# Rope on even and odd tiles without a shuffle, and TensorE's side work behind every second score step

## The chip, the cores and the metric

The kernel runs on one core of one Trainium2 chip. The metric is the device time of one execution in microseconds (us). The three runs of the kernel before took 2365.91, 2367.55 and 2371.05 us; their median is 2367.55 us.

## The reference

A macaron block on x of shape (32 samples, 512 positions, 256 features): half a routed feed-forward layer, attention, half a feed-forward layer again. The change touches attention alone.

```python
def rotate_half(x):
    x1 = x[..., ::2]
    x2 = x[..., 1::2]
    return jnp.stack((-x2, x1), axis=-1).reshape(x.shape)
...
freqs = jnp.exp(-math.log(10000.0) * jnp.arange(0, DH, 2) / DH)      # DH = 16, 16 heads
angles = jnp.repeat(pos[:, None] * freqs[None, :], 2, axis=-1)
qkv = x @ Wqkv.T
...
q = cos * q + rotate_half(q) * sin
k = cos * k + rotate_half(k) * sin
scores = where(causal, q k^T / 4, -inf)
out = softmax(scores) @ v
return out @ Wo.T                                                    # x is added by the caller
```

## The kernel before, in words

`program` builds tables, then runs `ffn_phase`, `attention_phase`, `ffn_phase`, one after the other. Only `attention_phase` (from L504) and the tables that `kernel` makes on the host differ after the change.

**Slots.** Attention goes through the samples in a software pipeline written out by hand. A slot is one group G of four heads of one sample; a sample s has four slots, g = 0 to 3. In its `slot` function each engine has its own list for the slot, and the engines meet only in semaphores. In slot G, TensorE computes what the row maxima need of group G (`max_scores`, L883), the transposed scores of group G-2 (`scores`, L907), probabilities times V of group G-3 (`probs_v` with kt 1, 3, 2, L927) and the first such product of group G-2 (kt 0). A slot has 11 steps n. Steps 0 to 9 have one score step into one of two banks `st_ps`; steps 0 to 10 have one maximum step into one of three banks `mx_ps` (`MX_BANK`). Score step c waits for the exponential c-2 (its bank), and maximum step n for the maximum that used its bank before: step 2 for maximum 0, 3 for 1, 5 for 2, 6 for 3, 8 for 5, 9 for 6, 10 for 7, and in the next slot 0 for 8 and 1 for 9.

**The turn.** At step 1 `turn_maxima` (L876, matmul at L880) transposes the maxima of the group before. It waits for `max_done` 11 G: all 11 maxima of that slot. ScalarE copies the result (`mneg`, L843), and a DMA writes it as a row into the query stack.

**VectorE** reduces each maximum step (`maxima`, L753), in order, and has between them: `begin_rope` (L722), `rope_low` (L730), `normalise_output` (L758: a reciprocal and a product), the statistics of the sample after next (L99 to L111, in slot 2 behind maximum 1), `low_of` (L774) of the transposed input and of the transposed attention output, and `add_residual` (L803). **ScalarE** computes ten exponentials (`exps`, L818) and has copies between them: the high halves of rope (`rope_high`, L820), of the transposed input and output (`high_of`, L828), V (`v_copy`, L860), and `o32` (L848), which `turn_output` (L982) waits for. **GpSimd** masks the probabilities in four instructions a slot (L675), and in `rope` (L678) makes the sine product (L681) and the sum (L685) of one tile. **SyncE** issues all DMAs in order: it writes the rotated queries and keys as fp16 high and low halves to a DRAM image (L646 for q, L655 for k) once `qk_lo` says that they are there, and reads each image back into the stacks in six requests (`read_stack`, L603, issued at L608). The maximum step 0 of slot 0 waits for the new sample's q and k stacks.

**Rope before.** The q and k of the next sample are four PSUM tiles t = 0 to 3 (q, q, k, k), each 128 features x 512 positions, two projected in slot 0, two in slot 1 (`project_qk`, L944, two halves of three matmuls each). Even and odd features stand beside each other in the partitions. VectorE multiplies the tile by the cosine and shuffles neighbouring partitions into `swapped`:

```python
nc.vector.tensor_tensor(by_cos[t % 2][:], x_ps[t % 2][:], cos_t[:], ALU.mult)
nc.vector.stream_shuffle(swapped[t % 2][:], x_ps[t % 2][:], [i ^ 1 for i in range(32)]).then_inc(rope_in, 1)
```

GpSimd multiplies `swapped` by a signed sine and adds. ScalarE rounds the sum to fp16 (L824), VectorE takes the rest (L734).

**TensorE's other work before** (`slot`, L1016): a half projection (slots 0 and 1; a V projection, L960, in slot 2) behind steps 0, 1, 4 and 5, the turn behind 1, three `probs_v` behind 2, `turn_output` behind 5, `probs_v` kt 0 behind 8. In slot 3 the transposes of the input (L973) stand behind 0, the transposes of the output (`transpose_o`, L990) behind 4, and two output projections each (`project_o`, L1004) behind 9 and 10.

Of the kernel before, what the change touches and what calls it, by code (L numbers as in the profile page):

```python
# [503 lines left out]
def attention_phase(nc, tab, src, dst, cos, sin):  # L504
# [10 lines left out]
    with ExitStack() as ctx:  # L515
# [13 lines left out]
        swapped = [sb(f"swapped{i}", [P, T], F32) for i in range(2)]  # L529
# [27 lines left out]
        xT_lo, qk_done, rope_in, sin_done = sem("xT_lo"), sem("qk_done"), sem("rope_in"), sem("sin_done")  # L557
        rope_done, qk_hi, qk_lo, v_done = sem("rope_done"), sem("qk_hi"), sem("qk_lo"), sem("v_done")
# [40 lines left out]
        def _(sp):  # L599
# [69 lines left out]
        def _(pool):  # L669
# [8 lines left out]
            def rope(n, t):  # L678
                idx = 4 * n.b + t
                pool.wait_ge(rope_in, idx + 1)  # L680
                nc.gpsimd.tensor_tensor(by_sin[t % 2][:], swapped[t % 2][:], sin_t[:], ALU.mult).then_inc(sin_done, 1)  # L681

                wait(pool, qk_lo, idx - 1)
                pool.wait_ge(sin_done, idx + 1)
                nc.gpsimd.tensor_tensor(rotated[t % 2][:], by_cos[t % 2][:], by_sin[t % 2][:], ALU.add).then_inc(rope_done, 1)  # L685
# [3 lines left out]
            def slot(s, g):  # L689
# [4 lines left out]
                if g < 2 and sample(s + 1):  # L694
                    rope(s + 1, 2 * g)
# [17 lines left out]
                if g < 2 and sample(s + 1):  # L713
                    rope(s + 1, 2 * g + 1)
# [3 lines left out]
        def _(dve):  # L718
# [3 lines left out]
            def begin_rope(n, t):  # L722
# [4 lines left out]
                nc.vector.tensor_tensor(by_cos[t % 2][:], x_ps[t % 2][:], cos_t[:], ALU.mult)  # L727
                nc.vector.stream_shuffle(swapped[t % 2][:], x_ps[t % 2][:], [i ^ 1 for i in range(32)]).then_inc(rope_in, 1)  # L728
# [49 lines left out]
            def slot(s, g):  # L778
                G = 4 * s.b + g
                for n in range(11):  # L780
                    if group(G):
                        maxima(s, g, n)
                    if g in (1, 2) and sample(s + 1) and n in (0, 3):
                        rope_low(s + 1, 2 * (g - 1) + (n == 3))
                    if group(G - 3) and n == 5:
                        normalise_output(s, g)
                    if g < 2 and sample(s + 1) and n in (2, 6):
                        begin_rope(s + 1, 2 * g + (n == 6))
# [5 lines left out]
                    if g == 3 and sample(s + 2) and n in (1, 2):  # L794
                        low_of(xT.lo, xT.hi, s + 2, n - 1, xT_hi, xT_lo)
                    if g == 3 and sample(s + -1) and n in (5, 7):
                        low_of(oT.lo, oT.hi, s + -1, int(n == 7), oT_hi, oT_lo)
# [14 lines left out]
        def _(act):  # L812
# [12 lines left out]

            act.wait_ge(consts_set, 2)
# [5 lines left out]
            def slot(s, g):  # L832
                G = 4 * s.b + g
                for n in range(10):
                    if group(G - 2):
                        exps(G, [n])
                    if g in (1, 2) and sample(s + 1) and n in (0, 2):
                        rope_high(s + 1, 2 * (g - 1) + (n == 2))
# [5 lines left out]
                    if group(G - 3) and n == 3:  # L844
# [4 lines left out]
                    if g == 3 and sample(s + 2) and n in (0, 1):  # L849

                        wait(act, v_done, 2 * (s + 2).b)
                        high_of(xT.hi, s + 2, n, xT_done, xT_hi)
                    if g == 2 and sample(s + 1) and n in (4, 7):
                        v_copy(s + 1, int(n == 7))
                    if g == 3 and sample(s + -1) and n in (4, 5):

                        wait(act, o_done, 2 * (s + -1).b)
                        high_of(oT.hi, s + -1, n - 4, oT_done, oT_hi)
# [13 lines left out]
        def _(pe):  # L872
# [143 lines left out]
            def slot(s, g):  # L1016
# [4 lines left out]
                before = group(G - 3)  # L1021
                for n in range(11):
# [4 lines left out]
                    if n == 2 and before:  # L1027
                        probs_v(s, g, 3, 1, 1)
                    if n == 1 and group(G - 1):
                        turn_maxima(s, g)  # L1030
                    if n == 2 and before:
# [78 lines left out]
```

## Time and profile before

| what | value |
|---|---|
| median of three runs | 2367.55 us |
| time of the profiled execution | 2366.41 us |
| its span, first to last instruction | 2364.7 us |
| busy, TensorE matmuls | 2146.5 us, 91% |
| busy, VectorE | 1919.6 us, 81% |
| busy, ScalarE | 1358.4 us, 57% |
| busy, GpSimd | 1276.5 us, 54% |
| mean granted TensorE clock | 0.975 |
| rope cosine product, shuffle (L727, L728), means | 678, 733 ns |

A busy matmul is not a matmul at its peak: the records of successive matmuls overlap, because each record has its drain in it. So below, work is priced by the distance from one start to the next, not by durations; the same holds for VectorE and ScalarE, where a record of 0.68 us is followed 0.60 us after its start by the next.

### The profile page before, as it was taken

What the parts mean: (1) busy time and instruction counts of PE and PEld (TensorE: products, weight loads), DVE (VectorE), ACT (ScalarE), POOL (GpSimd) and SP (SyncE); (2) the same over time, 40 slices, a digit from 0 to 9 for tenths busy, and PEclk for the clock granted to TensorE, in tenths of its full rate; (3) what the DMA queues carried; (4) which work ended last, traced back from release to release, by engine and by line L of the source; (5) the groups of instructions that cost most, each with busy time, mean ns of one, the idle gap of its engine ahead of it and who ended that gap; (6) DMA issues with size and microseconds to landing.
All of it is one profiled execution on the core that took longest, in us unless ns stands there. A gap on an engine that the chain in (4) does not pass through costs nothing. (4 is left out here: it accounts for less than half of the span.)

```text
span 2364.7 us, 53376 instructions
## 1 busy us (share of the span) xinstructions
PE 2146.5 (91%) x18188; PEld 1163.7 (49%) x18188; DVE 1919.6 (81%) x3961; ACT 1358.4 (57%) x2567; POOL 1276.5 (54%) x1459
## 2 busy tenths in 40 slices
PE   2999999589999999999999999999999986999999
PEld 1666666324444444444444444444444433666666
DVE  4777777469989998998998999899899855777776
ACT  2555555136666676666666666666666663455453
POOL 3666666335545554554554555455455425666664
PEclk9999999679999999999999999999999987999999
DMA  5566666333444454444454445444444413666664
GB/s 157 179 200 200 202 202 202 97 66 89 94 96 91 94 102 94 90 96 89 98 96 92 91 97 101 91 90 97 94 99 95 77 37 128 201 201 200 202 201 163
DMA packets 280350, 295.31 MB, mean 125 GB/s; under 512 B 45744, under 2 KB 263184, under 8 KB 280080
## 3 DMA queue, kind: packets, MB, share of 16 engines
q1 hardware_dynamic: 279536, 290.85, 48.6%
q8 instruction: 146, 2.39, 0.5%
q14 instruction: 124, 1.02, 0.2%
q10 hardware_dynamic: 544, 1.05, 0.1%
HBM read 140.08 MB, written 83.89 MB: 95 GB/s over the span
## 5 line engine op out<-in xcount | busy, mean ns | idle before, releaser
L818 ACT ACTIVATE at_probs<-at_st_ps 128x512 f32<-128x512 f32 x1280 | 748.1, 604 | 468.7 <-PE at_st_ps L923 462.1
L753 DVE TENSOR_REDUCE at_mx<-at_mx_ps 128x1 f32<-128x512 f32 (+3 forms) x1408 | 838.0, 633 | 142.9 <-PE at_mx_ps L905 142.9
L675 POOL TENSOR_SCALAR_AFFINE_SELECT at_probs<-at_probs 128x512 f32<-128x512 f32 x512 | 319.0, 635 | 679.2 <-ACT at_probs L818 675.4
L923 PE MATMUL at_st_ps<-at_q_stack,at_k_stack 49*128 49x512 f16 (+3 forms) x2048 | 461.3, 303 | 73.0 <-ACT at_probs L818 70.9
L900 PE MATMUL at_mx_ps<-at_k_stack,at_q_stack 48*128 48x512 f16 (+3 forms) x2048 | 493.8, 304 | 21.0 <-DMA at_k_stack<-qk_image 11.5
L431 ACT ACTIVATE f_h<-f_h_ps,f_b1s 128x512 f32<-128x512 f32 x256 | 176.0, 688 | 358.6 <-PE f_h_ps L473 347.1
L923 PEld LDWEIGHTS at_st_ps<-at_q_stack,at_k_stack 49*128 49x128 f16 x2048 | 136.6, 94 | 462.1 <-ACT at_probs L818 338.8
L905 PE MATMUL at_mx_ps<-mask,turn 64*128 64x128 bf16 (+2 forms) x1408 | 342.6, 243 | 0.0
L940 PE MATMUL at_pv_ps<-at_probs,at_v 128*32 128x512 f32 (+3 forms) x4096 | 333.7, 444 | 0.0
L489 PE MATMUL f_y_ps<-f_w2hi,f_hhi 128*128 128x256 f16 x1024 | 279.2, 273 | 0.0
L489 PE MATMUL f_y_ps<-f_w2lo,f_hhi 128*128 128x256 f16 x1024 | 279.2, 273 | 0.0
L489 PE MATMUL f_y_ps<-f_w2hi,f_hlo 128*128 128x256 f16 x1024 | 279.2, 273 | 0.0
L473 PE MATMUL f_h_ps<-f_xThi,f_w1hi 128*128 128x512 f16 x512 | 197.5, 386 | 31.2 <-DVE f_xTlo L380 31.1
L99 DVE BATCH_NORM_STATS2 f_stats<-f_x 128x6 f32<-128x256 f32 x256 | 89.8, 413 | 143.6 <-DMA f_x<-after_attention 72.7
L473 PE MATMUL f_h_ps<-f_xThi,f_w1lo 128*128 128x512 f16 x512 | 197.0, 385 | 0.0
L473 PE MATMUL f_h_ps<-f_xTlo,f_w1hi 128*128 128x512 f16 x512 | 196.6, 384 | 0.0
L681 POOL TENSOR_TENSOR at_by_sin<-at_swapped,at_sin 128x512 f32<-128x512 f32 x128 | 175.4, 1370 | 35.8 <-DVE at_swapped L728 35.8
L900 PEld LDWEIGHTS at_mx_ps<-at_k_stack,at_q_stack 48*128 48x128 f16 x2048 | 158.6, 94 | 68.5 <-DVE at_mx L753 38.7
L685 POOL TENSOR_TENSOR at_rotated<-at_by_cos,at_by_sin 128x512 f32<-128x512 f32 x128 | 180.6, 1411 | 19.1 <-POOL at_by_sin L681 0.4
L389 DVE TENSOR_TENSOR f_hlo<-f_h,f_hhi 128x512 f16<-128x512 f32 x256 | 172.0, 728 | 19.0 <-ACT f_hhi L432 18.9
L340 POOL TENSOR_TENSOR f_res<-f_x,f_b2q 128x1024 f32<-128x1024 f32 x64 | 150.8, 2357 | 64.6 <-DMA after_ffn<-f_res 31.6
L327 POOL TENSOR_SCALAR f_xn<-f_x,f_ve,f_rstd 128x256 f32<-128x256 f32 x256 | 169.7, 674 | 13.0 <-issue 12.1
(117 smaller groups left out, 3903.1 us busy)
## 6 DMA issues: line engine op xcount, KB each, us to landing
at_q_stack<-qk_image SPq DMA_DIRECT2D x192, 128.0 KB, 4.5
at_k_stack<-qk_image SPq DMA_DIRECT2D x192, 128.0 KB, 4.7
f_x<-in_x SPq DMA_DIRECT2D x32, 512.0 KB, 5.6
f_w1hi<-w_hi SPq DMA_DIRECT2D x128, 128.0 KB, 2.5
f_w1lo<-w_lo SPq DMA_DIRECT2D x128, 128.0 KB, 2.2
f_b2s<-in_b SPq DMA_DIRECT2D x128, 128.0 KB, 3.8
f_w2hi<-w_hi SPq DMA_DIRECT2D x128, 128.0 KB, 4.2
f_w2lo<-w_lo SPq DMA_DIRECT2D x128, 128.0 KB, 4.3
```

Of the source, the lines that this page charges most:

```text
L431: nc.scalar.activation(h32[j][:], h_ps[j][:], ACT.Gelu, bias=bias).then_inc(gelu_done, 1)
L473: ins = nc.tensor.matmul(h_ps[j][:], w, v, start=(n == 0), stop=(n == 3 * NC - 1))
L489: ins = nc.tensor.matmul(y_ps[t // 2][:, t % 2, :], v, w, start=(n == 0), stop=(n == 11))
L675: nc.gpsimd.affine_select(out=ap, in_=ap, compare_op=ALU.is_ge, fill=0.0, base=0, pattern=[[0, d] for d in dims] + [[1, P]], channel_multi ...
L681: nc.gpsimd.tensor_tensor(by_sin[t % 2][:], swapped[t % 2][:], sin_t[:], ALU.mult).then_inc(sin_done, 1)
L685: nc.gpsimd.tensor_tensor(rotated[t % 2][:], by_cos[t % 2][:], by_sin[t % 2][:], ALU.add).then_inc(rope_done, 1)
L753: nc.vector.tensor_reduce(o_ap, i_ap, AX_X, ALU.max).then_inc(max_done, 1)
L818: nc.scalar.activation(probs[:, c, :], st_ps[c % 2][:], ACT.Exp, scale=DH ** -0.5).then_inc(exp_done, 1)
L900: nc.tensor.matmul(bank[:, at * w:at * w + w], q_stack[s.par][rows, j + a, i * P:(i + 1) * P], k_stack[s.par][rows, j + a, 0:w], start=(at ...
L905: nc.tensor.matmul(last, tab.turn[const, :], over.broadcast_to([HP, nh, P]), start=False, stop=True).then_inc(mx_done, 1)
L923: ins = nc.tensor.matmul(bank[:, col:col + T - q0], k_stack[ss.par][rows, j + ha, kt * P:(kt + 1) * P], q_stack[ss.par][rows, j + ha, q0:T ...
L940: ins = nc.tensor.matmul(pv_ps[32 * a:32 * a + 32, kt * P:T], v[ss.par][:, kt, head_of(sg, a), :], p, start=(kt == 0), stop=(nth == 3), ti ...
```

## The change

Four edits. (1) The host orders the q and k columns of the weight so that one tile has all even features and the next all odd ones; angles, sine and the read pattern of the stacks follow. The shuffle goes; ScalarE copies the PSUM tile to SBUF (`rope_raw`) once VectorE's cosine product has read it. (2) GpSimd makes both sine products of a pair (`rope_sin`) and, behind the slot's last mask, a difference and a sum (`rope_sums`). (3) TensorE's other work stands behind steps 1, 3, 5, 7 and 9. (4) The other engines' places in the slot are moved to suit.

```diff
-        swapped = [sb(f"swapped{i}", [P, T], F32) for i in range(2)]
+        raw = [sb(f"raw{i}", [P, T], F32) for i in range(2)]
...
-                        img = image[2 * part + lo].rearrange("(j a r) n -> a r j n", a=2, r=DH)[par]
+                        img = image[2 * part + lo].rearrange("(r j a) n -> a r j n", a=2, r=DH)[par]
...
-            def rope(n, t):
+            def rope_sin(n, t):
                 idx = 4 * n.b + t
                 pool.wait_ge(rope_in, idx + 1)
-                nc.gpsimd.tensor_tensor(by_sin[t % 2][:], swapped[t % 2][:], sin_t[:], ALU.mult).then_inc(sin_done, 1)
...
+                wait(pool, rope_done, 4 * n.b + t // 2 * 2)
+                nc.gpsimd.tensor_tensor(by_sin[t % 2][:], raw[t % 2][:], sin_t[:], ALU.mult).then_inc(sin_done, 1)
+
+            def rope_sums(n, u):
+                pool.wait_ge(sin_done, 4 * n.b + 2 * u + 2)
+                for e, op in ((0, ALU.subtract), (1, ALU.add)):
+
+                    wait(pool, qk_lo, 4 * n.b + 2 * u - 1 + e)
+                    nc.gpsimd.tensor_tensor(rotated[e][:], by_cos[e][:], by_sin[1 - e][:], op).then_inc(rope_done, 1)
...
                 if g < 2 and sample(s + 1):
-                    rope(s + 1, 2 * g)
+                    rope_sin(s + 1, 2 * g)
+                    rope_sin(s + 1, 2 * g + 1)
...
                 if g < 2 and sample(s + 1):
-                    rope(s + 1, 2 * g + 1)
+                    rope_sums(s + 1, g)
...
-                nc.vector.tensor_tensor(by_cos[t % 2][:], x_ps[t % 2][:], cos_t[:], ALU.mult)
-                nc.vector.stream_shuffle(swapped[t % 2][:], x_ps[t % 2][:], [i ^ 1 for i in range(32)]).then_inc(rope_in, 1)
+                nc.vector.tensor_tensor(by_cos[t % 2][:], x_ps[t % 2][:], cos_t[:], ALU.mult).then_inc(cos_done, 1)
...
-                    if g in (1, 2) and sample(s + 1) and n in (0, 3):
+                    if g in (1, 2) and sample(s + 1) and n in (7, 10):
...
-                    if group(G - 3) and n == 5:
+                    if group(G - 3) and n == 6:
                         normalise_output(s, g)
-                    if g < 2 and sample(s + 1) and n in (2, 6):
+                    if g < 2 and sample(s + 1) and n in (2, 8):
...
-                    if g == 3 and sample(s + 2) and n in (1, 2):
+                    if g == 3 and sample(s + 2) and n in (2, 3):
...
-                    if g == 3 and sample(s + -1) and n in (5, 7):
+                    if g == 3 and sample(s + -1) and n in (6, 8):
...
+            def rope_raw(n, t):
+                idx = 4 * n.b + t
+                act.wait_ge(cos_done, idx + 1)
+
+                wait(act, sin_done, idx - 1)
+                nc.scalar.activation(raw[t % 2][:], x_ps[t % 2][:], ACT.Copy).then_inc(rope_in, 1)
...
-                    if g in (1, 2) and sample(s + 1) and n in (0, 2):
-                        rope_high(s + 1, 2 * (g - 1) + (n == 2))
+                    if g in (1, 2) and sample(s + 1) and n in (6, 8):
+                        rope_high(s + 1, 2 * (g - 1) + (n == 8))
+                    if g < 2 and sample(s + 1) and n in (3, 9):
+                        rope_raw(s + 1, 2 * g + (n == 9))
...
-                    if group(G - 3) and n == 3:
+                    if group(G - 3) and n == 4:
...
-                    if g == 3 and sample(s + 2) and n in (0, 1):
+                    if g == 3 and sample(s + 2) and n in (1, 2):
...
-                    if g == 2 and sample(s + 1) and n in (4, 7):
+                    if g == 2 and sample(s + 1) and n in (3, 8):
...
-                    if g == 3 and sample(s + -1) and n in (4, 5):
+                    if g == 3 and sample(s + -1) and n in (5, 6):
...
+                    if n == 1:
+                        if group(G - 1):
+                            turn_maxima(s, g)
+                        if g < 2 and nxt:
+                            project_qk(s + 1, 2 * g, half=False)
+                            project_qk(s + 1, 2 * g, half=True)
+                        if g == 2 and nxt:
+                            project_v(s + 1, 0)
+                            project_v(s + 1, 1)
+                        if g == 3 and aft:
+                            transposes(s + 2)
+                    if n == 3 and before:
                         probs_v(s, g, 3, 1, 1)
...
                         probs_v(s, g, 3, 2, 3)
                         probs_v(s, g, 3, 3, 2)
...
+                    if n == 5:
+                        if g < 2 and nxt:
+                            project_qk(s + 1, 2 * g + 1, half=False)
+                        if g == 2 and nxt:
+                            project_v(s + 1, 2)
+                        if g == 3 and old:
+                            transpose_o(s + -1, s)
+                        if before:
+                            turn_output(s, g)
+                    if n == 7:
+                        if g < 2 and nxt:
+                            project_qk(s + 1, 2 * g + 1, half=True)
+                        if g == 2 and nxt:
+                            project_v(s + 1, 3)
+                    if n == 9 and run:
                         probs_v(s, g, 2, 0, 0)
...
+                    if g == 3 and old and n >= 9:
                         project_o(s + -1, 2 * (n - 9))
                         project_o(s + -1, 2 * (n - 9) + 1)
```

## Rows read from the trace of the kernel before

**Rows 1.** TensorE's timeline: the turns of the maxima, slots 2, 3, 0, 1, 2.

```profile
1005.46 0.28 PE L880 MATMUL at_mx_ps<-ident,at_mx 128*16 128x128 f32 x1
...
1016.44 0.28 PE L880 MATMUL at_mx_ps<-ident,at_mx 128*16 128x128 f32 x1
...
1029.30 0.28 PE L880 MATMUL at_mx_ps<-ident,at_mx 128*16 128x128 f32 x1
...
1039.78 0.28 PE L880 MATMUL at_mx_ps<-ident,at_mx 128*16 128x128 f32 x1
...
1050.83 0.28 PE L880 MATMUL at_mx_ps<-ident,at_mx 128*16 128x128 f32 x1
```

**Rows 2.** VectorE's timeline in the same stretch (start us, us, instruction).

```profile
1006.80 1.39 DVE L99 BATCH_NORM_STATS2 at_stats<-at_x 128x6 f32<-128x256 f32 x4
...
1009.00 1.28 DVE L753 TENSOR_REDUCE at_mx<-at_mx_ps 128x1 f32<-128x512 f32 x2
...
1028.27 0.69 DVE L753 TENSOR_REDUCE at_mx<-at_mx_ps 128x1 f32<-128x512 f32 x1 [0.51 <-PE at_mx_ps L905]
...
1039.92 1.20 DVE L734 TENSOR_TENSOR at_qk_lo<-at_rotated,at_qk_hi 128x512 f16<-128x512 f32 x1
...
1042.25 0.67 DVE L727 TENSOR_TENSOR at_by_cos<-at_x_ps,at_cos 128x512 f32<-128x512 f32 x1
...
1042.85 0.72 DVE L728 STREAM_SHUFFLE at_swapped<-at_x_ps 128x512 f32<-128x512 f32 x1
1043.47 0.67 DVE L753 TENSOR_REDUCE at_mx<-at_mx_ps 128x1 f32<-128x512 f32 x1
1044.07 0.81 DVE L734 TENSOR_TENSOR at_qk_lo<-at_rotated,at_qk_hi 128x512 f16<-128x512 f32 x1
1044.80 1.01 DVE L753 TENSOR_REDUCE at_mx<-at_mx_ps 128x1 f32<-128x384 f32 x2
1045.73 0.24 DVE L765 RECIPROCAL at_inverse<-at_pv_ps 128x16 f32<-128x16 f32 x1
...
1046.42 0.55 DVE L753 TENSOR_REDUCE at_mx<-at_mx_ps 128x1 f32<-128x384 f32 x1
```

**Rows 3.** TensorE's timeline between the turns.

```profile
1019.18 1.06 PE L1001 MATMUL at_x_ps<-ident,at_on 128*128 128x128 f32 x8
...
1024.41 0.28 PE L1010 MATMUL at_x_ps<-wo_hi,at_oT_hi 128*128 128x256 f16 x1
...
1027.79 0.39 PE L923 MATMUL at_st_ps<-at_q_stack,at_k_stack 49*128 49x512 f16 x1
...
1040.64 0.39 PE L923 MATMUL at_st_ps<-at_q_stack,at_k_stack 49*128 49x512 f16 x1
...
1042.45 0.39 PE L923 MATMUL at_st_ps<-at_q_stack,at_k_stack 49*128 49x512 f16 x1
...
1044.13 0.66 PE L987 MATMUL at_pv_ps<-ident,at_o 128*128 128x128 f32 x4
...
1046.51 0.28 PE L923 MATMUL at_st_ps<-at_q_stack,at_k_stack 49*128 49x256 f16 x1 [0.52 <-ACT at_probs L818]
```

**Rows 4.** ScalarE's timeline: the exponential of step 3, the copy behind it.

```profile
1042.93 0.60 ACT L818 ACTIVATE at_probs<-at_st_ps 128x512 f32<-128x512 f32 x1
1043.42 0.59 ACT L848 ACTIVATE at_o<-at_pv_ps 128x512 f32<-128x512 f32 x1
```

**Rows 5.** GpSimd's timeline: a sine product.

```profile
1039.31 1.27 POOL L681 TENSOR_TENSOR at_by_sin<-at_swapped,at_sin 128x512 f32<-128x512 f32 x1
```

**Rows 6.** SyncE's timeline: the k reads, a second image write.

```profile
1018.31 2.87 SPq L608 DMA_DIRECT2D at_k_stack<-qk_image  x6
...
1045.37 0.46 SPq L646 DMA_DIRECT2D qk_image<-at_qk_lo  x1
```

**Rows 7.** SyncE's waits, 1016 to 1030 us (total, times, longest).

```profile
SPq L67 <- DMA at_k_stack<-qk_image: 5.0, 1, 5.0
```

**Rows 8.** DMA issues, 1010 to 1030 us (KB each, median us to landing).

```profile
qk_image<-at_qk_lo SPq DMA_DIRECT2D x1, 256.0 KB, 4.9
```

More of the change, by code:

```diff
@@ L557, in attention_phase @@
         xT_lo, qk_done, rope_in, sin_done = sem("xT_lo"), sem("qk_done"), sem("rope_in"), sem("sin_done")
+        cos_done = sem("cos_done")
         rope_done, qk_hi, qk_lo, v_done = sem("rope_done"), sem("qk_hi"), sem("qk_lo"), sem("v_done")
@@ L1021, in slot @@
                 before = group(G - 3)
+                nxt, aft, old = sample(s + 1), sample(s + 2), sample(s + -1)
                 for n in range(11):
@@ L1026, in slot @@
                         max_scores(s, g, n)
-                    if n == 2 and before:
+                    if n == 1:
[9 more added lines that the diff above has]
+                            transposes(s + 2)
@@ L1028, in slot @@
+                    if n == 3 and before:
                         probs_v(s, g, 3, 1, 1)
-                    if n == 1 and group(G - 1):
-                        turn_maxima(s, g)
-                    if n == 2 and before:
                         probs_v(s, g, 3, 2, 3)
                         probs_v(s, g, 3, 3, 2)
-                    if n == 5 and before:
-                        turn_output(s, g)
-                    if g < 2 and sample(s + 1) and n in (0, 1, 4, 5):
-                        project_qk(s + 1, 2 * g + (n > 3), half=(n in (1, 5)))
@@ L1038, in slot @@
-                    if g == 2 and sample(s + 1) and n in (0, 1, 4, 5):
-                        project_v(s + 1, (0, 1, 4, 5).index(n))
-                    if g == 3 and sample(s + 2) and n == 0:
-                        transposes(s + 2)
-                    if run and n == 8:
+                    if n == 5:
[7 more added lines that the diff above has]
+                            turn_output(s, g)
@@ L1043, in slot @@
+                    if n == 7:
[4 more added lines that the diff above has]
+                    if n == 9 and run:
                         probs_v(s, g, 2, 0, 0)
-                    if g == 3 and sample(s + -1) and n == 4:
-                        transpose_o(s + -1, s)
-                    if g == 3 and sample(s + -1) and n >= 9:
+                    if g == 3 and old and n >= 9:
@@ L1084 @@
     freqs = np.exp(np.float32(-np.log(10000.0)) * np.arange(0, DH, 2, dtype=np.float32) / np.float32(DH)).astype(np.float32)
-    angles = np.arange(T, dtype=np.float32)[None, :] * freqs[(np.arange(P) % DH) // 2][:, None]
-    sign = np.where(np.arange(P) % 2 == 0, -1.0, 1.0).astype(np.float32)[:, None]
+    angles = np.arange(T, dtype=np.float32)[None, :] * freqs[np.arange(P) // H][:, None]
+    halves = np.arange(D).reshape(H, DH // 2, 2).transpose(2, 1, 0).reshape(-1)
+    columns = np.concatenate([halves, D + halves, 2 * D + np.arange(D)])
     ins = {
         "x": L0_attn_x,
-        "WqkvT": np.asarray(L0_attn_Wqkv).T,
+        "WqkvT": np.asarray(L0_attn_Wqkv).T[:, columns],
         "WoT": np.asarray(L0_attn_Wo).T,
@@ L1097 @@
         "cos": np.cos(angles).astype(np.float32),
-        "sin": (np.sin(angles) * sign).astype(np.float32),
+        "sin": np.sin(angles).astype(np.float32),
     }
```

17 lines of the change are left out of this document (7 added, 10 removed).

## The prediction

> **What bounds the kernel now.** Feed-forward is untouched, so I read attention alone, one period of the steady state, and in it first TensorE's timeline at the turns of the maxima [rows 1]. Five turns give four slots: 10.98 us (slot 2), 12.86 (slot 3), 10.48 (slot 0) and 11.05 (slot 1), 45.37 us in all. The turn is the right mark, since it needs all of VectorE's maxima of the slot before and everything on TensorE is queued behind it. Next comes VectorE's timeline [rows 2]. By starts, a maximum over 512 columns costs 0.60 us (1043.47 to 1044.07), over 384 columns 0.47 (two from 1044.80 to 1045.73), the cosine product 0.60, the shuffle 0.62, the normalisation 0.69 (1045.73 to 1046.42), the statistics 2.20 (1006.80 to 1009.00). From 1039.92 to 1046.42 no row has an idle bracket: in slot 1 VectorE never rests. Its work there is seven maxima at 0.60 and four at 0.47 (6.08), normalisation 0.69, two cosine products and two shuffles (2.44), two low parts at 0.60 (1.20) and some 0.53 extra for the slow one (below): 10.94 against the slot's 11.05. So VectorE sets slot 1, and slot 2 with its statistics nearly. Slots 0 and 3 belong to TensorE, which has two sorts of stall: at score step 8 it sits idle 0.52 us for an exponential [rows 3] (its last row), once a slot in all four, and VectorE idles at step 0 of slot 0 (0.51 us [rows 2]), because TensorE is late.
>
> **The change part by part.**
>
> *Shuffle out.* 4 x 0.62 = 2.48 us of VectorE a period. Only the two of slot 1 (1.24 us) lie where VectorE sets the end.
>
> *Raw copy in.* Four ScalarE copies of a PSUM tile, 0.49 us each by the distance from exponential to `o32` copy [rows 4] (1042.93 to 1043.42). Copy 0 of a pair stands behind exponential 3, where TensorE has 1.4 us of `probs_v` before step 4: hidden. Copy 1 stands behind exponential 9 and waits for the cosine product, late in the slot. It holds up only GpSimd; its sine product (1.27 us [rows 5]) and three masks then come about 2.7 us after the turn's slot begins, and the `probs_v` that need them follow one after another from 2.2 us on, of which only the first mask (by some 1.5) must be there at 2.2. I take nothing; bound 0 to 0.5 us a slot in slots 1 and 2.
>
> *TensorE's new order.* I lay it out from a turn (time 0). Turn and three matmuls take 0.86 us (1039.78 to 1040.64 [rows 1, 3]), three more 0.66: step 2 at 1.52, step 3 at 1.74. Step and `probs_v` take 1.81 (1040.64 to 1042.45): step 4 at 3.55. A maximum can start 0.48 after its step (1027.79 to 1028.27 [rows 2, 3]). VectorE is free for the new slot at -0.14 (a maximum ends 0.69 after its start and the turn follows 0.05 behind, against its 0.60 by starts). Now `turn_output` waits for the `o32` copy, which has moved behind exponential 4: before, step 3 to `turn_output` was 1.68 us (1042.45 to 1044.13), and the same chain now starts at step 4, so `turn_output` comes at 5.23, though the half projection in front of it ends at 4.8. With its own 0.5 and a change of block of 0.1, step 6 is at 5.82 and maximum 6 at 6.30.
>
> *Slot 0.* Behind maximum 6 VectorE still has maximum 6 (0.47), normalisation (0.69), maximum 7 (0.47), 8, a cosine product and 9 (1.80): maximum 10 starts at 9.73 and the turn comes 0.74 later, at **10.47** (before 10.48).
>
> *Slot 1.* The same and one low part (0.60): **11.07** (before 11.05). The 1.24 us of the shuffles are there, but as holes: VectorE is done with maxima 0 and 1 at 1.06 and gets maximum 2 at 2.00; it is done with 5 at about 5.0 and gets 6 at 6.30.
>
> *Slot 2.* The low part of tile 1 now starts as the slot begins, while GpSimd still runs the sine product that the late copy 1 released. [rows 2, 5] show what that costs: GpSimd began at 1039.31 and ended at 1040.58, the low part began at 1039.92, lasted 1.20 us and took 1.13 by starts (1042.25 less two maxima). So low part to 0.99, maxima 0 and 1 to 2.19, statistics to 4.39, maximum 2 to 4.99. TensorE: step 3 waits for maximum 1 (2.33), step 4 at 4.14, step 5 waits for maximum 2 (5.13), V projection and `turn_output` to 6.71 = step 6. Maximum 6 at 7.19, then 3.43 as in slot 0 with the low part in the cosine product's place, and 0.74: **11.36** (before 10.98). The Trainium skill, "SBUF — State Buffer", section "Who interferes with whom", says that a VectorE instruction with two SBUF inputs and a GpSimd one that reads SBUF exclude each other for the whole instruction; the row agrees (the low part ended 0.54 us after GpSimd). By that rule the wait would be the whole rest of the sine product, 0.2 us more than I count, some 6 us on the kernel.
>
> *Slot 3.* Low part to 0.46, maxima 0 and 1 to 1.66. Transposes take 1.0 (eight of them at 1019.18 [rows 3]): step 2 at 1.20, step 3 for maximum 1 at 1.80, step 4 at 3.61. VectorE: maximum 2 from 1.68, first `xT` low part, maximum 3, second low part, which ends at 4.16; so `transpose_o` starts at 4.3, then `turn_output`, step 6 at 5.90, step 7 at 6.12. Nothing stands behind step 7 here. ScalarE: exponential 6 from 6.38 to 6.98, the second `oT` copy, exponential 7 from 7.36 to 7.96: step 8 waits to 7.04 and step 9 to 8.02, two stalls of 0.6 where one of 0.5 was. The first `probs_v` fits before 9.5. The output projections need the second `oT` low part, which VectorE starts behind maximum 8: maximum 6 at 6.38, normalisation, low part, 7, 8 to 9.21, low part ended at 9.89. They start at 10.04. From there to the next step 0 is 3.38 us (1024.41 to 1027.79), thus 13.42, and to the turn 0.65 (1.51 before, less the projection between): **14.07** (before 12.86, which had one half projection where the new slot has the transposes, +0.3).
>
> *The k chain.* The low part of the last k tile moved from slot 2's step 3 to its step 10. It ends at 0.54 of slot 3; the second image write follows 0.5 later (1044.88 to 1045.37 [rows 2, 6]) and lands after 4.9 us [rows 8], at 5.9; the six reads last from 1018.31 to the end of SyncE's wait at 1026.18 [rows 6, 7], 7.87 us. Stack there at 13.8, with 0.15 for TensorE 14.0, against 13.42. The write's 4.9 was measured behind six q reads; they are farther ahead now, so it may land a microsecond sooner, and then the chain costs nothing. I take 0.3 a period, bounds 0 to 0.9. The reads' rows in DRAM are the same 1 KB pieces at another stride; no row prices that, bound -1 to +1 us on the reads. The q chain moves likewise from slot 1 into slot 2, with a slot of slack left.
>
> **Sum.** 10.47 + 11.07 + 11.36 + 14.07 + 0.3 = 47.27, or +1.9 us a period. 31 samples have the full pattern: +59 us. Ramp and tail, bounded at -5 to +5, I count as nothing. On the profiled execution's 2366.4 us (span 2364.7) that is 2425; the median of the runs lies 1.1 above it, so **2426 us**, 2.5% slower.
>
> **The rivals.**
>
> *Faster: TensorE stays ahead and the holes don't open.* Place: slot 1, before maximum 6. For it: each pair of steps now has a block behind it, so the 0.52 us stall at step 8 goes in slots 0, 1 and 2, TensorE changes blocks one time less a slot (three in slot 3), and VectorE loses 2.48 us. If maximum 6 came at 5.0 instead of 6.3, slot 1 would lose its 1.24, slots 0 and 3 about 0.7 each: 2.6 a period, 82 us, 2284 us. It decides where the hole before maximum 6 is under about 0.4 us. Against it: the `o32` copy behind exponential 4. The Trainium skill, "Perfetto Trace Analysis", section "Optimizing Scalar/DVE Operations", advises moving work from a saturated VectorE to ScalarE; whether it holds here hangs on these holes, since slot 1 has that saturated engine. Chance 0.17.
>
> *No change.* Slot 3 loses only half of its 1.2, slot 2 nothing, the k chain nothing, and slots 0 and 1 gain 0.3 each by a steadier feed: within 5 us of before. Chance 0.07.
>
> *A little slower.* The stalls of slot 3 don't add up (ScalarE's copies get ahead), so that it takes 12.9, and the rest holds: 45.8, +0.4 a period, 2380 us. Chance 0.15.
>
> *The k chain bounds slot 3 outright.* Write at 4.9, reads a microsecond longer by the new stride: stack at 15, +1.6 in place of +0.3, 3.2 a period, 2466 us. The reads had 1.6 us of slack before (landed at 1026.18, needed at 1027.79). Chance 0.12.
>
> **How the numbers follow.** The forecast has 0.49. Faster by over 0.2%, about what a measurement of this kernel can tell from no change (4.7 us): 0.17; within it 0.07; slower 0.49 + 0.15 + 0.12 = 0.76. The range leaves out the faster case and a fifth of the k chain's: 2363 to 2470 us.
>
> **What would show it.** Turns at 10.5, 11.1, 11.4 and over 14 us; VectorE idle about 1.3 us for L905 before maximum 6 in slots 0 and 1, and 0.9 before maximum 2 in slot 1; `turn_output` (L987's counterpart) waiting for the `o32` copy by 0.4; a low part of 1.2 us or more at the start of slot 2; in slot 3 two stalls for exponentials and one of the output projection for the low part; step 0 of slot 0 waiting for the k stack. I am wrong if slot 1 is under 10.5 us, or slot 3 under 13.

## The result, and the profile after

The changed kernel takes 2543.95 us (2543.58 to 2547.47, four runs) against 2367.3 us before: ratio 1.0752, 95% interval 1.0737 to 1.0766. The profiled execution has a span of 2541.9 us against 2364.7. The forecast was 2426 us with a range to 2470: the sign was right, the size was not. The change costs 177 us, three times the 59 foreseen.

TensorE's timeline shows where, by the same marks as [rows 1] (`turn_maxima` is L895 now). The turns stand in the order slot 0, 1, 2, 3, 0:

```profile
992.13 0.28 PE L895 MATMUL at_mx_ps<-ident,at_mx 128*16 128x128 f32 x1
...
1002.56 0.28 PE L895 MATMUL at_mx_ps<-ident,at_mx 128*16 128x128 f32 x1 [0.15 <-DVE at_mx L759]
...
1014.57 0.28 PE L895 MATMUL at_mx_ps<-ident,at_mx 128*16 128x128 f32 x1 [0.15 <-DVE at_mx L759]
...
1029.16 0.28 PE L895 MATMUL at_mx_ps<-ident,at_mx 128*16 128x128 f32 x1
...
1043.31 0.28 PE L895 MATMUL at_mx_ps<-ident,at_mx 128*16 128x128 f32 x1
```

| slot | before | forecast | after |
|---|---|---|---|
| 0 | 10.48 | 10.47 | 10.43 |
| 1 | 11.05 | 11.07 | 12.01 |
| 2 | 10.98 | 11.36 | 14.59 |
| 3 | 12.86 | 14.07, and 0.3 for the k chain | 14.15 |
| period | 45.37 | 47.27 | 51.18 |

5.8 us a period times 31 is 180 us, which is the whole difference of 177. Slots 0 and 3 came out near the forecast; slots 1 and 2 are 4.2 us worse than it.

VectorE's timeline in slots 1 and 2 holds both answers (compare [rows 2]):

```profile
1004.55 0.69 DVE L759 TENSOR_REDUCE at_mx<-at_mx_ps 128x1 f32<-128x512 f32 x1 [0.85 <-PE at_mx_ps L920]
1006.40 0.69 DVE L734 TENSOR_TENSOR at_by_cos<-at_x_ps,at_cos 128x512 f32<-128x512 f32 x1 [1.17 <-POOL at_rotated L691]
...
1014.44 1.41 DVE L740 TENSOR_TENSOR at_qk_lo<-at_rotated,at_qk_hi 128x512 f16<-128x512 f32 x1
1015.77 1.27 DVE L759 TENSOR_REDUCE at_mx<-at_mx_ps 128x1 f32<-128x512 f32 x2
1016.97 1.39 DVE L99 BATCH_NORM_STATS2 at_stats<-at_x 128x6 f32<-128x256 f32 x4
1018.39 0.39 DVE L103 TENSOR_TENSOR at_pair<-at_stats 128x4 f32<-128x4 f32 x1
1018.71 0.15 DVE L104 TENSOR_TENSOR at_pair<-at_stats 128x4 f32<-128x4 f32 x1
1018.78 1.23 DVE L105 TENSOR_TENSOR at_pair<-at_stats 128x4 f32<-128x4 f32 x1
1020.05 0.56 DVE L107 TENSOR_SCALAR at_ve<-at_pair 128x4 f32<-128x4 f32 x1
...
1020.86 2.21 DVE L759 TENSOR_REDUCE at_mx<-at_mx_ps 128x1 f32<-128x512 f32 x4
```

In slot 1 VectorE stands idle 1.17 us before the cosine product of tile 2, until GpSimd's difference has read the buffer that the product is to write; the raw copy behind it, and on ScalarE the exponentials and the `o32` copy behind that, are late by as much. In slot 2 the low part takes 1.33 us by starts, and the statistics 3.89 (1016.97 to 1020.86) instead of 2.20; two operations of 128 x 4 elements take 1.23 and 0.56 us, where 0.17 was the rule. GpSimd's timeline shows what ran meanwhile:

```profile
1014.03 1.27 POOL L684 TENSOR_TENSOR at_by_sin<-at_raw,at_sin 128x512 f32<-128x512 f32 x1 [4.68 <-ACT at_raw L837]
1015.25 2.27 POOL L676 TENSOR_SCALAR_AFFINE_SELECT at_probs<-at_probs 128x512 f32<-128x512 f32 x3
1017.49 2.50 POOL L691 TENSOR_TENSOR at_rotated<-at_by_cos,at_by_sin 128x512 f32<-128x512 f32 x2
1019.95 0.63 POOL L676 TENSOR_SCALAR_AFFINE_SELECT at_probs<-at_probs 128x512 f32<-128x512 f32 x1
```

The low part lies on the sine product, the statistics on the two sums and the mask behind them: L105 ends at 1020.01, 0.02 us after the sums, and L107 at 1020.61, 0.03 after the mask. TensorE's step 5 waits for the maximum behind the statistics, and then its matmuls are slow:

```profile
1021.60 0.33 PE L915 MATMUL at_mx_ps<-at_k_stack,at_q_stack 48*128 48x384 f16 x1 [2.08 <-DVE at_mx L759]
...
1024.79 0.42 PE L982 MATMUL at_x_ps<-qkv_hi,at_xTlo 128*128 128x256 f16 x1
1025.00 0.42 PE L982 MATMUL at_x_ps<-qkv_lo,at_xThi 128*128 128x256 f16 x1
```

By windows of the same slot (busy time and count of each engine, then the granted clock, the DMA share and GB/s):

```profile
1018.57:1020.57 2.00, 0.94 (x14) 0.27 (x6) 1.97 (x5) 1.47 (x4) 2.00 (x3) 1.00 0.07 24
1020.57:1022.57 2.00, 0.97 (x8) 0.71 (x9) 1.97 (x8) 0.66 (x2) 1.35 (x3) 0.99 0.94 167
1022.57:1024.57 2.00, 2.00 (x14) 1.12 (x12) 0.75 (x3) 0.24 (x1) 1.85 (x4) 0.50 1.21 128
1024.57:1026.57 2.00, 2.00 (x18) 1.25 (x16) 1.90 (x6) 1.45 (x4) 0.47 (x1) 0.66 0.76 84
```

TensorE is busy 0.94 and 0.97 us of two windows of 2 us, then its granted clock is 0.50 (1.2 GHz), and a V projection's matmul takes 0.21 us from start to start instead of 0.11. This happens in every period (22 times between 600 and 1700 us); in the kernel before no slot of the steady state has it.

### The profile page after: what moved, and what is told of

Its sections match the earlier page's. It is cut to its first block and busy times, and to the rows that moved or that the text cites. A ratio compares the mean times of both kernels' runs of the same rounds, so it can differ in the third digit from the quotient of the medians.

```text
span 2541.9 us, 53437 instructions
## 1 busy us (share of the span) xinstructions
PE 2204.5 (87%) x18188; PEld 1195.2 (47%) x18188; DVE 1900.4 (75%) x3705; ACT 1403.3 (55%) x2695; POOL 1267.3 (50%) x1459
## 3 DMA queue, kind: packets, MB, share of 16 engines
q10 hardware_dynamic: 544, 1.05, 0.1%
## 5 line engine op out<-in xcount | busy, mean ns | idle before, releaser
L759 DVE TENSOR_REDUCE at_mx<-at_mx_ps 128x1 f32<-128x512 f32 (+3 forms) x1408 | 848.6, 634 | 302.6 <-PE at_mx_ps L920 302.3
L824 ACT ACTIVATE at_probs<-at_st_ps 128x512 f32<-128x512 f32 x1280 | 728.0, 599 | 493.1 <-PE at_st_ps L938 485.8
L676 POOL TENSOR_SCALAR_AFFINE_SELECT at_probs<-at_probs 128x512 f32<-128x512 f32 x512 | 340.5, 686 | 584.1 <-ACT at_probs L824 583.7
L915 PE MATMUL at_mx_ps<-at_k_stack,at_q_stack 48*128 48x384 f16 (+3 forms) x2048 | 485.6, 309 | 89.8 <-DVE at_mx L759 71.5
L938 PE MATMUL at_st_ps<-at_q_stack,at_k_stack 49*128 49x512 f16 (+3 forms) x2048 | 432.5, 309 | 47.8 <-ACT at_probs L824 46.7
L684 POOL TENSOR_TENSOR at_by_sin<-at_raw,at_sin 128x512 f32<-128x512 f32 x128 | 162.2, 1267 | 323.8 <-ACT at_raw L837 320.3
L432 ACT ACTIVATE f_hhi<-f_h_ps,f_b1s 128x512 f16<-128x512 f32 x256 | 174.2, 681 | 0.0
```

Source lines behind the costliest of these rows:

```text
L432: nc.scalar.activation(h[s % 2].hi[:, j, :], h_ps[j][:], ACT.Gelu, bias=bias).then_inc(gelu_done, 1)
L676: nc.gpsimd.affine_select(out=ap, in_=ap, compare_op=ALU.is_ge, fill=0.0, base=0, pattern=[[0, d] for d in dims] + [[1, P]], channel_multi ...
L759: nc.vector.tensor_reduce(o_ap, i_ap, AX_X, ALU.max).then_inc(max_done, 1)
L824: nc.scalar.activation(probs[:, c, :], st_ps[c % 2][:], ACT.Exp, scale=DH ** -0.5).then_inc(exp_done, 1)
L915: nc.tensor.matmul(bank[:, at * w:at * w + w], q_stack[s.par][rows, j + a, i * P:(i + 1) * P], k_stack[s.par][rows, j + a, 0:w], start=(at ...
L938: ins = nc.tensor.matmul(bank[:, col:col + T - q0], k_stack[ss.par][rows, j + ha, kt * P:(kt + 1) * P], q_stack[ss.par][rows, j + ha, q0:T ...
```

## The experiments

Fourteen kernels ran. Each is timed against the kernel before on the same chip, and its ratio is to that. A difference to the changed kernel goes across chips, on which the kernel before differs by up to 5 us. Slot lengths are from each run's own turns.

**Four cosine buffers**, the changed kernel otherwise:

```diff
-        by_cos = [... for i in range(2)]
+        by_cos = [... for i in range(4)]
-                wait(dve, rope_done, idx - 1)      # and by_cos[t % 2], by_cos[e]
+                wait(dve, rope_done, idx - 3)      # and by_cos[t], by_cos[2 * u + e]
```

> Four buffers for the cosine product in place of two, so that the cosine product of tile 2 no longer waits for GpSimd's difference and sum of tiles 0 and 1. Theory (the buffer is what slot 1 waits for: 1.17 us idle before L734, and with it the raw copy, exponential 4, the o32 copy and the turn of the output): slot 1 falls from 12.0 to 11.1 us by the turns, slot 2 stays at 14.6, and the kernel gets faster by 31 x 0.9 = 28 us, to about 2516. Rival (the wait only fills a hole that is there anyway, since VectorE stands idle before maximum 6 too): slot 1 stays at 12.0 and the time within 5 us of 2544.

2499.03 us, ratio 1.0565 (1.0529 to 1.0602), 45 us less than the changed kernel. Slot 1 is 11.04 us: the buffer was all of what slot 1 lost, and the forecast of 11.07 is what comes out without it. Most of the rest of the gain is the clock: its low stretch now comes in about every second period (11 where the changed kernel has 22). That gives two slots 2 of one execution, one without a low stretch and one with it (windows from turn to turn):

```profile
1001.28:1015.00 13.72, 10.71 (x105) 5.50 (x105) 12.75 (x27) 8.11 (x19) 11.43 (x15) 1.00 0.57 98
...
1050.36:1064.90 14.54, 12.22 (x105) 6.07 (x105) 12.64 (x27) 8.04 (x18) 11.17 (x15) 0.88 0.49 92
```

The two differ by 0.82 us, but not in the clock alone: the statistics take 4.09 us in the first and 3.89 in the second, so the low stretch costs about 1.0 us. The pair shows another thing: in the first slot TensorE stands still for 2.28 us before step 5 and its clock stays at 1.00, in the second for 2.08 us and it falls. The standstill alone doesn't decide whether the clock falls; what does was not found.

**Statistics behind maximum 5**: in VectorE's slot, `g == 2 ... and n == 1` becomes `n == 5`.

> The statistics of the next sample stand behind maximum 5 of slot 2 instead of behind maximum 1, after GpSimd's difference and sum are done. Theory (VectorE's small operations on two SBUF tiles are held by GpSimd's sums, 3.9 us instead of 2.2, TensorE then stands still for 2.1 us and its clock falls to 1.2 GHz for 3.4 us): statistics take 2.2 us again, the clock stays at 1.00 through the stage, slot 2 falls from 14.6 to about 12, and the kernel to about 2464 (2.6 x 31 = 80 us less). Rival (the place of the statistics doesn't matter, VectorE has the same work): slot 2 falls by the 1.7 us of the lock at most with no change of the clock, 2490 to 2500. Rival (worse): GpSimd gets the statistics too late, the transposes of slot 3 wait for xn, and slot 3 grows by what slot 2 gains.

2478.64 us, 1.0482 (1.0449 to 1.0514). Slot 2 is 12.28 us, slots 1 and 3 stay at 12.0 and 14.1, and the clock is 1.00 from 600 to 1500 us. So the theory held, with 65 of the 80 us.

**A block into the standstill**: in slot 2 `project_v(s + 1, 2)` moves from step 5 to step 4.

> In slot 2 the third V projection stands behind step 4 instead of step 5, so TensorE has 0.7 us of work inside its longest standstill (2.1 us) and the same work in all. Theory (half of what slot 2 lost beyond the lock is the clock): if the shorter standstill of 1.4 us keeps the clock at 2.4 GHz, slot 2 falls by about 2.4 us (0.7 that is now hidden and some 1.7 at the low clock), and the kernel to about 2470. Rival (the clock costs nothing because VectorE sets the slot): slot 2 falls by 0.7 at most, about 2522, whatever the clock does. If the clock still falls, it says nothing on its price, and about 0.7 us a period is expected.

2502.74 us, 1.0584 (1.0549 to 1.0619). The clock still falls in about a third of the periods (7 stretches between 600 and 1700 us where the changed kernel has 22), and here the pair is clean. The statistics take 3.9 us and TensorE stands still for 1.22 us before step 5 in both slots:

```profile
1003.36:1017.28 13.92, 12.47 (x104) 5.98 (x105) 12.63 (x27) 8.04 (x18) 11.16 (x15) 0.88 0.56 97
1053.89:1066.81 12.92, 10.97 (x105) 5.41 (x105) 12.47 (x27) 8.10 (x19) 11.44 (x15) 1.00 0.59 104
```

So the clock had a price of its own, though smaller than the 1.7 expected: 1.0 us in slot 2. The hidden work came on top with 0.6 us, since 12.92 stands against 13.53 for a slot 2 of the changed order at full clock (next run).

**The `o32` copy before exponential 4** instead of behind it:

```diff
                 for n in range(10):
+                    if group(G - 3) and n == 4:
+                        ...                        # the o32 copy, moved up unchanged
                     if group(G - 2):
                         exps(G, [n])
```

> ScalarE's o32 copy stands before exponential 4 instead of behind it, all else as changed. Theory of the prediction (the turn of the output waits for this copy, 0.4 us in slots 0 and 3 and with it maximum 6, and VectorE then sets the rest of the slot): slots 0 and 1 fall by 0.4 us each, the kernel by 25 to 35 us, to about 2515. Rival (exponential 4 gets late by the same 0.5 us, and score step 6 waits for it): no gain in any slot, 2544 within 10 us.

2486.49 us, 1.0517 (1.0483 to 1.055). Slots 0 and 1 fall to 9.97 and 11.52, by 0.46 and 0.49, and VectorE's hole before maximum 6 goes from 1.19 to 0.70 us: this copy made 0.5 of it, and the rest is left. The gain is more than 30 us since the low stretches halve here too (11 of 22). Slot 2 is 14.59 us with one and 13.53 without, at the same statistics (3.89) and the same standstill (2.08): 1.06 us for the clock.

**TensorE's new order alone**, on the kernel before with its shuffle and its four separate sums (TensorE's `slot` of the changed kernel, the other engines' places to suit, second low part behind maximum 7):

> The kernel before (its rope with shuffle and four separate sums) with only TensorE's new order and the places of the other engines that go with it; the second tile's low part stands behind maximum 7. Theory (the order alone costs what the prediction counted, holes before maxima 2 and 6 and slot 3's stalls; the statistics aren't locked out here): slots of about 11.1, 11.9, 11.4 and 14.1 us, 48.5 in all against 45.4, and about 2460. Rival (the order is no loss, rope is all of it): 2350 to 2385.

2493.02 us, 1.054 (1.0513 to 1.0566). Slots 11.06, 12.63, 12.04 and 13.7. The order by itself costs about 130 us. More than expected, since its late second tile puts the low part on GpSimd's work in slots 1 and 2 (1.63 us each where a free one takes 0.68), but its statistics take the usual 2.2 us.

**The new rope alone**, with TensorE's `slot` of before:

> The changed kernel's rope (no shuffle, raw copy, sums in pairs behind the masks, low parts behind maxima 7 and 10) with TensorE's order of before and the other places of before; the raw copy of the second tile stands behind exponential 7. Theory (rope alone costs the wait for the cosine buffer, 1 us in slot 1, and the statistics locked out by the sums, up to 1.7 us in slot 2, and gives back 2.5 us of VectorE): slots of about 10.4, 11.3, 12.5 and 12.9, 47 in all, about 2420. Rival (the rope edit is a gain and only TensorE's order loses): under 2360.

2457.19 us, 1.0391 (1.0365 to 1.0418). Slots 10.88, 10.88, 12.28 and 13.9 to 15.5. The new rope by itself costs about 95 us. Not as foreseen, slot 3 suffers: with TensorE's old order step 0 of slot 0 waits for the k stack (in four of six periods, 3.7 us in all and 1.5 the longest), which the kernel after does not. And slot 0 grew, since the raw copy stood before the `o32` copy. Alone, the order and the rope cost 130 and 95 us, together 177: they don't add up.

**The three repairs together** (buffers, statistics, `o32` copy) on the changed kernel:

> The changed kernel with four cosine buffers, the statistics behind maximum 5, and the o32 copy before exponential 4 together. Theory (three separate causes that add up, by the slots of the single runs: 10.0, 10.6, 11.9 and 14.1 us): 46.6 a period, about 2405, still slower than before by what slot 3 loses (14.1 against 12.9). Rival (they overlap, since the clock's low stretch is counted in each): about 2440.

2406.59 us, 1.0171 (1.0145 to 1.0198), slots 9.97, 10.57, 12.28 and 14.06. The slots are what the single runs gave one by one, so the three causes are separate. They make 133 of the 177 us, each kernel against the one before on its own chip.

**The old order with the rope mended** (buffers, statistics behind maximum 5):

> TensorE's order of before, rope without the shuffle, four cosine buffers and the statistics behind maximum 5. Theory (without the two waits that the new rope brought, the 2.5 us of VectorE that the shuffle took are a gain in slots 1 and 2, which VectorE sets): slots of about 10.3, 10.3, 11.0 and 12.9, 44.5 in all, about 2340. Rival (TensorE is within 0.5 us of VectorE in every slot, and its stall at step 8 stays): no more than 0.3 us a period gained, 2358 to 2368.

2455.87 us, 1.039 (1.0362 to 1.0417): the expectation failed. Slots 10.88, 10.88, 13.09 and mostly 12.85. In slots 0 and 1 `turn_output` waits 0.36 us for the `o32` copy, which stands behind the raw copy; in slot 2 TensorE stands 0.98 us before the transposes, for `xn`, since the statistics had become late for the old order.

**The old order with the statistics in slot 1** and `o32` ahead of the raw copy:

> TensorE's order of before, rope without shuffle, four cosine buffers, the o32 copy ahead of the raw copy, and the statistics in slot 1 behind maximum 5 (the input of that sample is requested in slot 0). Theory (the run with the old order lost by the o32 copy queued behind the raw copy, 0.4 us in slots 0 and 1, and by the late xn, 2.3 us in slot 2; with both gone TensorE sets slots 0 and 3 as before and VectorE's 2.5 us are a gain in slots 1 and 2): slots of 10.5, 10.8, 10.6 and 12.9, 44.8 a period against 45.4, about 2347, faster than the kernel before. Rival (the low parts still fall on GpSimd's sine product and sums at the slots' starts): slot 2 stays at 11 or above, 2360 to 2375.

2460.04 us, 1.0401 (1.0376 to 1.0425): the expectation failed again. Slot 0 is 10.46 now, but slot 1 is 12.35 (the statistics hold up the second cosine product, and ScalarE's exponential 8 behind the raw copy), slot 2 11.2, slot 3 14.0 (step 2 stands 0.40 us for maximum 0, which is late behind a low part of 1.14 us; in one period of six slot 3 is 15.75, with a wait of 1.74 us for the k stack).

**The same move in the three-repair kernel**:

> The same move of the statistics into slot 1 in the changed kernel with four cosine buffers and the early o32 copy (TensorE's new order). Theory (VectorE sets slots 1 and 2 in this order, so the 2.2 us only change their slot, less the hole before maximum 6 that they fill): slot 1 goes from 10.6 to about 11.9, slot 2 from 12.3 to about 10.5, slots 0 and 3 stay at 10.0 and 14.1, 46.5 a period, about 2402: no better than with the statistics behind maximum 5 of slot 2. Rival (slot 2 was held by GpSimd more than by VectorE's work): under 2390.

2433.56 us, 1.0287 (1.0263 to 1.0311), slots 9.97, 12.19, 11.3 and 14.06. Worse than foreseen, since slot 2 keeps 11.3.

**One wait more.** The changed kernel, where GpSimd's sums of the k tiles wait for the statistics:

```diff
                 pool.wait_ge(sin_done, 4 * n.b + 2 * u + 2)
+                if u == 1 and sample(n + 1):
+                    pool.wait_ge(stats_done, n.b + 2)
```

> The changed kernel with one wait more and nothing else: GpSimd's difference and sum of the k tiles wait until VectorE's statistics of slot 2 are done. Theory (the two engines shut each other out on operations with two SBUF inputs, and the statistics lose 1.7 us by it, TensorE then stands still, and its clock falls): the statistics take 2.2 us by starts instead of 3.9, slot 2 falls from 14.6 to about 12.3, few or no low stretches of the clock are left, and a kernel that only waits more is 50 to 75 us faster, about 2480. Rival (the small operations of the statistics are slow for another reason, such as their waits on each other): they still take 3.9 us, and the time is 2544 or more.

2476.88 us, 1.0476 (1.0454 to 1.0498): 67 us faster by waiting. VectorE's timeline has the statistics at 2.20 us again (1043.62 to 1045.82):

```profile
1043.62 1.39 DVE L99 BATCH_NORM_STATS2 at_stats<-at_x 128x6 f32<-128x256 f32 x4
...
1045.20 0.16 DVE L105 TENSOR_TENSOR at_pair<-at_stats 128x4 f32<-128x4 f32 x1
1045.39 0.17 DVE L107 TENSOR_SCALAR at_ve<-at_pair 128x4 f32<-128x4 f32 x1
...
1045.82 2.21 DVE L761 TENSOR_REDUCE at_mx<-at_mx_ps 128x1 f32<-128x512 f32 x4
```

TensorE's turns put slot 2 at 11.84 us, and the clock has no low stretch between 600 and 1700 us:

```profile
1041.22 0.28 PE L897 MATMUL at_mx_ps<-ident,at_mx 128*16 128x128 f32 x1 [0.15 <-DVE at_mx L761]
...
1053.06 0.28 PE L897 MATMUL at_mx_ps<-ident,at_mx 128*16 128x128 f32 x1 [0.23 <-DVE at_mx L761]
```

Of all runs this one leaves the least room for another cause. Instructions and places are the same; only GpSimd's sums, and the mask behind them, no longer lie on VectorE's small operations. Slot 2's 14.59 is thus 11.84 and 2.75 for the exclusion and the clock together; by the pair of slots in the run with the early `o32` copy, 1.69 and 1.06. Slot 3 gives 0.19 back (14.34): GpSimd is later, and the low part that opens slot 3 takes 1.05 us by starts where it took 0.88.

**Slot 3 with its old order**, in the three-repair kernel:

> The changed kernel with four cosine buffers, the statistics behind maximum 5 and the early o32 copy (as in the run of the three together), and in slot 3 alone TensorE's order and the other engines' places of before. Theory (slot 3 loses 1.2 us by its new order): slot 3 goes from 14.1 to about 13.0, less the transposes, which now stand ahead of the turn and are added to slot 2; the sum of slots 2 and 3 falls by 1.0, and the kernel from 2407 to about 2375. Rival (the late low part and the k stack hold slot 3, whatever the order): slots 2 and 3 together fall by less than 0.4, 2395 to 2410.

2391.75 us, 1.0107 (1.0086 to 1.0127), 15 us less than with the new order in slot 3. Slots 2 and 3 together are 25.5 to 26.6 us, 25.9 in the mean of six periods, where they were 26.4. The outcome lies between the two expectations: going back to the old order there takes 0.5 us off slot 3's loss of 1.2. What holds the rest was not settled. The k stack is among it (TensorE waited for it 0.9 us in two places in 300 us), and this run has a wait of its own, 0.4 us a period for `xn` before the early transposes.

**One block of the kernel before moved**: the slot's second half projection from behind step 5 to behind step 7, in slots 0 to 2, and the second cosine product behind maximum 8:

> The kernel before with one block of TensorE's moved: the second half projection of the slot (in slot 2 the fourth V projection) from behind step 5 to behind step 7, and with it the second cosine product and shuffle behind maximum 8 and the second V copy behind exponential 8. Theory (the 0.5 us standstill at step 8 is for want of work behind step 7; VectorE stays fed, since the turn of the output isn't held up and no projection is put together): slot 0 loses 0.5 us, slot 2 up to 0.4, slot 1 nothing because VectorE sets it, slot 3 nothing: 0.5 to 0.9 us a period, 2338 to 2352. Rival (VectorE is left without work behind step 5 and gets it back too late, as in the changed kernel): no gain, 2362 to 2380.

2360.68 us, 0.9981 (0.9971 to 0.9991), between the two expectations: a gain, but a small one. Slots 10.08, 10.72, 11.35 and 12.86: slots 0 and 1 gain 0.4 and 0.3, slot 2 gives 0.4 back.

**The same in slots 0 and 1 alone:**

```diff
-                    if g < 2 and sample(s + 1) and n in (0, 1, 4, 5):
-                        project_qk(s + 1, 2 * g + (n > 3), half=(n in (1, 5)))
+                    if g < 2 and sample(s + 1) and n in (0, 1, 4, 7):
+                        project_qk(s + 1, 2 * g + (n > 3), half=(n in (1, 7)))
```

> The kernel before with the second half projection behind step 7 instead of step 5 in slots 0 and 1 alone, and the second cosine product and shuffle behind maximum 8; slot 2 as before. Theory (slot 2's 0.4 us in the run with all three slots came from its own V projection and V copy): slots of 10.1, 10.7, 11.0 and 12.9, 0.7 a period less than before, about 2343, faster than both kernels. Rival (slot 2's loss came from slot 1, whose late second tile pushes GpSimd's sum and the low part into the statistics): slot 2 stays at 11.3, 2355 to 2362.

2356.23 us, 0.9957 (0.9944 to 0.9971): faster than both kernels, by 0.4% and 7%. The rival's numbers came: slot 2 stays at 11.3 with its own order untouched (TensorE's turns, slots 0, 1, 2):

```profile
1031.52 0.28 PE L880 MATMUL at_mx_ps<-ident,at_mx 128*16 128x128 f32 x1
...
1041.60 0.28 PE L880 MATMUL at_mx_ps<-ident,at_mx 128*16 128x128 f32 x1
...
1052.32 0.28 PE L880 MATMUL at_mx_ps<-ident,at_mx 128*16 128x128 f32 x1 [0.15 <-DVE at_mx L753]
...
1063.62 0.28 PE L880 MATMUL at_mx_ps<-ident,at_mx 128*16 128x128 f32 x1
```

So slot 2's V projection wasn't what lost. But the rival's mechanism isn't there either. VectorE's timeline from slot 2's first low part to slot 3's maximum 1, in the kernel before and in this one:

```profile
1050.97 0.67 DVE L734 TENSOR_TENSOR at_qk_lo<-at_rotated,at_qk_hi 128x512 f16<-128x512 f32 x1
...
1061.91 0.69 DVE L753 TENSOR_REDUCE at_mx<-at_mx_ps 128x1 f32<-128x512 f32 x1 [0.24 <-PE at_mx_ps L905]
```

```profile
1052.78 0.68 DVE L734 TENSOR_TENSOR at_qk_lo<-at_rotated,at_qk_hi 128x512 f16<-128x512 f32 x1
...
1063.73 0.69 DVE L753 TENSOR_REDUCE at_mx<-at_mx_ps 128x1 f32<-128x512 f32 x1 [0.24 <-PE at_mx_ps L905]
```

That is 10.94 and 10.95 us, with the low part at 0.60 and the statistics at 2.2 in both: VectorE loses nothing in slot 2. The mark has moved. Before, slot 2's turn (1050.83) came 0.14 us ahead of this low part; now (1052.32) it comes 0.46 ahead, since TensorE no longer lags behind VectorE there, and so slot 2 reads 0.3 longer without being so. By the same measure on VectorE, from low part to low part, the gain sits in slot 1: 11.05 us before (1039.92 to 1050.97), 10.73 now.

## Why the prediction was right or wrong

*Shuffle out, and the holes.* Right. Slot 0 came at 10.43 against 10.47, and slot 1 at 11.04 against 11.07 once the buffer was out of the way. The run with the early `o32` copy shows the chain that was named: 0.46 and 0.49 us in slots 0 and 1 where 0.4 was reckoned. The faster rival needed a hole of under 0.4 us before maximum 6; the kernel after has 1.19 to 1.25 there.

*Raw copy in: "I take nothing; bound 0 to 0.5 us a slot".* Wrong, and the first step that failed. The text followed who waits for the raw copy, but not what the cosine product ahead of it waits for. Its buffer was free in good time before, because each tile's sum came before the next pair; with the sums moved behind the masks, the unchanged line `wait(dve, rope_done, idx - 1)` in `begin_rope` became a wait of 1.17 us. It is 0.97 us a period, 30 us in all (12.01 against 11.04).

*Slot 2.* The exclusion (two-input operations of VectorE and GpSimd's work keeping each other out) was named, but for one instruction, the low part at the slot's start (1.13 us taken, 1.33 measured). The step that failed is "statistics to 4.39", that is 2.20 us by [rows 2]: that row was read with GpSimd elsewhere, and the two sums now run from 2.92 to 5.4 us of the slot, straight over the statistics. It was never asked where the moved sums would lie. The statistics lost 1.69 us by it; with the clock it is 2.75 us by the run with one wait more, 85 us over 31 periods, of which slot 3 gave 6 back and the time of the whole kernel showed 67. The Trainium skill's rule ("SBUF — State Buffer", "Who interferes with whom"), that a VectorE instruction with two SBUF inputs contends with a GpSimd one that reads SBUF, was quoted for the low part at 0.2 us more, and this trace agrees: 1.33 against 1.13. It bears out the statistics too, whose L105 took 1.23 us and ended with GpSimd's sums. The rest of the miss, 11.84 against the forecast 11.36, is 0.1 us up to maximum 6, from the low part, and 0.3 behind it, where VectorE waits 0.24 us for the last maximum's step and the text had no wait.

*The clock* had no term at all. TensorE's standstill of 2.1 us is followed by 3.4 us at half clock in each period of the kernel after, at 1.0 to 1.06 us a time in slot 2: 31 to 33 us in all. It is part of the 2.75. Why half of such standstills passed without it in two of the runs stays open.

*Slot 3* was right in size (14.15 against 14.07), but only partly for the reasons given, and partly by luck. With the old order there the loss shrinks by 0.5 of 1.2 us and isn't gone. And its opening low part, taken at 0.60, took 0.88 (1029.02 to 1029.90), on a mask of GpSimd (1028.79 to 1029.43): in the run with four buffers slot 3 is 13.88 us where this low part takes 0.60 and 14.15 where it takes 0.87. So the steps as reckoned come to 13.88, and an exclusion that the text didn't have here filled the gap to 14.07.

*The k chain.* Forecast 0.3 us, nothing measured: the second write landed within 2.6 us (issued at 1030.47, the reads began at 1033.04) where 4.9 was taken, and the stack was there at about 1042.1 (the reads' issue and SyncE's wait of 5.3 behind it), half a microsecond before it was needed at 1042.66. The reads themselves were slower, 9.05 us where 7.87 was taken, so the two errors partly cancel. The chain does bind in some periods of the old-order runs. SyncE's issues show it:

```profile
1030.47 0.47 SPq L656 DMA_DIRECT2D qk_image<-at_qk_lo  x1
...
1033.04 3.75 SPq L609 DMA_DIRECT2D at_k_stack<-qk_image  x6
```

*Sum.* Forecast 47.27, measured 51.18: 0.97 for the buffer, 3.2 for slot 2, less 0.2 in slot 3 with its k term.

## What to carry to other kernels

When work is moved on one engine, ask of every instruction that keeps its place what its unchanged waits now wait for, buffers first: a `% 2` that was slack becomes a wait of the length of the move. And lay the moved work's span over the other engine of the pair VectorE and GpSimd: a moved sum costs nothing on its own engine and stops the neighbour's smallest operations. A hand schedule from one profile gave slot 0 to 0.1 us, and slot 3 with some luck; what it missed were the conditions under which its rows had been taken. When slots are read off one engine's marks, check a shift between neighbours on the engine that sets the pace: a mark that comes earlier makes one slot look shorter and the next longer.

## What the runs showed of the hardware

VectorE's operations of 128 x 4 elements on two SBUF tiles, 0.16 us alone, take up to 1.23 us while GpSimd runs a 128 x 512 sum, and end when it ends (1020.01 against 1019.99); one with a single input tile (L107) took 0.56 instead of 0.17 us on a mask. Making GpSimd wait made the kernel 67 us faster. After a standstill of TensorE of 2.1 us, with 1.9 us of busy time in the 4 us around it, the granted clock was 1.2 GHz for 3.4 us in every period of the kernel after; in the runs with four buffers and with the early copy, standstills of 2.28 and 2.08 us passed at full clock in about every second period. A low stretch cost slot 2 1.0 to 1.06 us, read off slots of one execution with the same statistics and the same standstill.
